# Shared places for the first expert's weights, the residual by the matrix unit and row stores ahead of the scan, in a two-layer kernel

## The reference, cut to what matters

```python
xn  = layernorm(x)                       # x: result of the first layer
x   = x + mamba(xn) + moe(xn)
mamba(r): y = scan over 1024 positions of h = exp(dt*A)*h + (dt*u)*B, y = sum(h*C), 16 states per channel
          return r + (y * silu(skip)) @ out_w.T          # r is the residual
moe(r):   logits = r @ gate_w + gate_b; two of 8 experts per token, softmax weights
          expert(r) = (silu(g) * h) @ w2 + b2 with h, g = split(r @ w1 + b1)
```

## Time and profile before

| | us |
|---|---|
| median of 3 runs (2567.91 to 2570.71) | 2570.66 |
| the profiled execution, its own time | 2571.51 |
| its span, first to last instruction | 2569.8 |
| DVE busy | 1967.2 |
| PE busy | 2128.3 |
| POOL busy | 1330.0 |

### The profile page before, as it was taken

The page is one execution under the profiler, slowest core; times in us unless marked ns, Lnnn a source line. Parts: engine busy times, 40 slices in busy tenths (PEclk is TensorE's granted clock), DMA queues, the critical chain, the costliest instruction groups (busy, mean ns, idle before and its releaser), DMA issues. The chain is left out here.

```text
span 2569.8 us, 34895 instructions
## 1 busy us (share of the span) xinstructions
PE 2128.3 (83%) x10642; PEld 1527.3 (59%) x10642; DVE 1967.2 (77%) x2692; ACT 1371.7 (53%) x2333; POOL 1330.0 (52%) x953
## 2 busy tenths in 40 slices
PE   2699999999976788788888888766599999999991
PEld 1578777787742233333333333332499999999991
DVE  6654566444536999989999999999498888888882
ACT  1322233322346766666666666743377777677760
POOL 1102222022224999999999999996024333433331
PEclk8899999999987999999999999999799999999996
DMA  8010011100121213131313131321466666666746
GB/s 263 17 42 16 25 41 41 41 25 16 41 74 59 103 62 113 66 109 74 113 60 116 61 112 62 105 82 66 173 226 220 208 230 233 217 210 227 236 138 206
DMA packets 117336, 290.84 MB, mean 113 GB/s; under 512 B 20788, under 2 KB 93892, under 8 KB 98452
## 3 DMA queue, kind: packets, MB, share of 16 engines
q1 hardware_dynamic: 102964, 271.31, 30.0%
q0 software_dynamic: 14304, 18.75, 3.6%
HBM read 239.21 MB, written 50.82 MB: 113 GB/s over the span
## 5 line engine op out<-in xcount | busy, mean ns | idle before, releaser
L1058 POOL TENSOR_TENSOR m_work<-m_ux,m_bb 128x1024 f32<-128x1024 f32 x256 | 601.7, 2370 | 37.3 <-DVE m_ux L1317 18.8
L1434 PE MATMUL m_y<-m_work,m_ident 128*128 128x512 f32 x1024 | 498.2, 609 | 1.5 <-DVE m_work L1347 1.5
L1204 ACT ACTIVATE m_da<-m_dl,m_A 128x512 f32<-128x512 f32 x512 | 347.9, 685 | 278.3 <-DVE m_hh L1339 277.5
L1748 PE MATMUL e_h<-e_xTh,e_w1h 128*128 128x256 f32 x1248 | 353.3, 283 | 17.1 <-DVE e_xTl L1684 17.1
L1748 PE MATMUL e_h<-e_xTl,e_w1h 128*128 128x256 f32 x1248 | 349.4, 280 | 0.0
L1748 PE MATMUL e_h<-e_xTh,e_w1l 128*128 128x256 f32 x1248 | 349.2, 280 | 0.0
L1347 DVE TENSOR_TENSOR m_work<-m_hh,m_cb 128x1024 f32<-128x1024 f32 x256 | 312.7, 1222 | 37.7 <-PE m_cb L1408 13.7
L1339 DVE TENSOR_TENSOR_SCAN m_hh<-m_da,m_carry,m_work 128x512 f32<-128x512 f32 x256 | 313.8, 1267 | 11.5 <-POOL m_work L1058 11.5
L1339 DVE TENSOR_TENSOR_SCAN m_hh<-m_da,m_work 128x512 f32<-128x512 f32 x256 | 298.4, 1207 | 14.7 <-POOL m_work L1058 14.5
L1434 PEld LDWEIGHTS m_y<-m_work,m_ident 128*128 128x128 f32 x1024 | 198.8, 194 | 161.8 <-issue 149.8
L281 POOL TENSOR_TENSOR small<-mv,eps_ln 128x4 f32<-128x4 f32 x17 | 3.4, 199 | 551.8 <-DVE mv L399 551.8
(11 more groups left out here) (263 smaller groups left out, 4755.9 us busy)
## 6 DMA issues: line engine op xcount, KB each, us to landing
e_w<-in_w SPq DMA_DIRECT2D x39, 2048.0 KB, 7.5
m_bb<-scratch_bT SPq DMA_DIRECT2D x64, 1024.0 KB, 4.6
e_w<-in_w SPq DMA_DIRECT2D x39, 1024.0 KB, 10.0
scratch_rec<-x1p SPq DMA_DIRECT2D x39, 260.0 KB, 8.1
e_xg<-scratch_rec SPq DMA_DIRECT2D x39, 260.0 KB, 2.7
e_b<-in_b SPq DMA_DIRECT2D x39, 128.0 KB, 3.0
xt<-in_x SPq DMA_DIRECT2D x9, 512.0 KB, 5.4
xres<-in_x SPq DMA_DIRECT2D x8, 512.0 KB, 4.8
```

The lines of the kernel that those rows point to most:

```text
L1058: pool.tensor_tensor(bx[:, u % NB], ux[q % 2][:, cols], slot.to_broadcast([P, HALF, T]), ALU.mult).then_inc(s_bx, 1)
L1204: act.activation(da[d % NA][:], dl[q % 2][:, e], ACT.Exp, scale=A[:, at:at + 1]).then_inc(s_exp, 1)
L1434: last = mm(y[:, i], ident[:], hc[:, u % 4, i], start=False, stop=(n % NST == NST - 1))
L1748: last = mm(hbank[m % HR][:, j], w[i][:, k, cols], x[i][:, k], start=(p == 0 and k == 0 and j == 0), stop=(p == 2 and k == KD - 1 and j == 1),
```

## The change

1. `mamba` places `xpad` and `w_si` in one tile `first`, which stays allocated for `experts`; the first expert tile's `w1` and `w2` take the same places. SP loads both at the end of `mamba`'s list, after their last reader. `experts` loads only rows, biases and the second tile's weights at its start.
2. The last output piece (O1 of chunk 7) goes to PSUM bank `da[0]` and to its own buffer `mo2`.
3. PE adds x1p to each output piece with an identity matmul; SP loads x1p for it (`load_res`) into the place of `xr`, so that the next `xr` is loaded later. `combine` becomes one copy from DRAM to DRAM.
4. The plan's exponential and matmuls move to slots (-2, 28) and (-2, 30). 14 of the 64 row stores come before the first step, the other 50 every fifth step.

```diff
+    PRE = 14
-        w_si = sb("w_si", [P, KD, 2 * E_IN])
+        first = dram["held"].enter_context(nc.sbuf_tensor("m_first", [P, KE * (PAD + 2 * T) + 2 * KD * E_IN], F32))
+        xpad = first[:, 0:KE * (PAD + 2 * T)].rearrange("p (e t) -> p e t", e=KE)
+        w_si = first[:, KE * (PAD + 2 * T):].rearrange("p (k n) -> p k n", k=KD)
+        xres = xr[:].rearrange("p k t -> p (k t)").rearrange("p (s d) -> p s d", d=D)
+            def load_res(p):
+                if p + 2 < NCH:
+                    wait_filled(sp, "SK3", p + 2)
+                if p > 0:
+                    wait_filled(sp, "O1", p - 1)
+                sp.dma_start(xres, dram["x1p"][p * T:(p + 1) * T, :].rearrange("(s p) d -> p s d", p=P)).then_inc(res_in, 16)
@@ SP, ahead of the steps
-            load_xr(1)
-            store_b(0)
             sp.wait_ge(s_d, D_STEPS)
...
+            sp.dma_start(tex0[:], dram["tex"][0:1, 0:1]).then_inc(tex0_in, 16)
             load_rows(0)
             load_rows(1)
+            load_xr(1)
+            store_b(0)
             load_b(0)
             load_b(1)
+            for j in range(2, PRE // TOPK + 1):
+                load_rows(j)
@@ SP, chunk q (load_rows becomes more_rows at the same places)
                 load_b(8 * q + 3)
-                load_rows(SUB * q + 2)
-                if q + 2 < NCH:
-                    load_xr(q + 2)
+                more_rows(32 * q + 0)
+                if q > 0:
+                    load_res(q - 1)
                 load_b(8 * q + 4)
                 if q > 0:
                     store_rows(q - 1, 0)
                     store_rows(q - 1, 1)
+                if q + 2 < NCH:
+                    if q > 0:
+                        wait_filled(sp, "O1", q - 1)
+                    load_xr(q + 2)
@@ SP, after the last chunk's list
+            sp.wait_ge(s_cv, NCH * KE)
+            wait_filled(sp, "SK3", NCH - 1)
+            sp.wait_ge(tex0_in, 16)
+            e = sp.value_load(tex0[0:1, 0:1], min_val=0, max_val=NE - 1)
+            sp.dma_start(first[:, 0:2 * KD * FF]..., dram["w1"][bass.ds(e * P, P), :, :]).then_inc(w_first, 16)
+            sp.dma_start(first[:, KE * (PAD + 2 * T):]..., dram["w2"][bass.ds(e * P, P), :, :]).then_inc(w_first, 16)
+            load_res(NCH - 1)
@@ POOL
-                    stores = [a // TOPK % 2 for a in range((q * NU + n + 2) // 4)]
+                    stores = [a // TOPK % 2 for a in range(PRE + (q * NU + n + 3) // 5)]
             pool.wait_ge(s_d, D_STEPS)
+            for a in range(PRE):
+                spread_rows(a)
             for u in range(AHEAD):
                 inputs(u)
-                if u % 4 == 2:
-                    spread_rows(u // 4)
+                if u % 5 == 2 and PRE + u // 5 < NPICK:
+                    spread_rows(PRE + u // 5)
@@ ACT and PE: the plan's parts
-                if (q, n) == (-1, 9):
+                if (q, n) == (-2, 28):
-                if (q, n) == (-1, 6):
+                if (q, n) == (-2, 30):
@@ PE, pieces O0 and O1
+                to = da[0] if (g, p) == ("O1", NCH - 1) else rb
                     pe.wait_ge(s_y1, 2 * p + 2)
+                    pe.wait_ge(res_in, 16 * (p + 1))
                     for s in (2 * j, 2 * j + 1):
+                        mm(to[:, at], ident[:], xres[:, s], start=(s % 2 == 0), stop=False, skip_group_check=True)
@@ experts
+            load_rows(0, 0)
             sp.dma_start(tex[:], dram["tex"]).then_inc(tex_in, 16)
...
             for t in range(2):
-                load_rows(t, t)
-                load_weights(t, t)
+                if t > 0:
+                    load_rows(t, t)
+                    load_weights(t, t)
+            act.wait_ge(w_first, 32)
+            dve.sem_inc(w_in[0], 16)
+            dve.sem_inc(w_in[0], 16)
@@ combine
+            sp.dma_start(out.rearrange("(p n) d -> p (n d)", p=P),
+                         dram["mo"][T:, :].rearrange("(p n) d -> p (n d)", p=P)).then_inc(out_done, 16)
```

More of the change, by code:

```diff
@@ L789, in mamba @@
         rb = ctx.enter_context(nc.psum_tensor("m_rb", [P, T], F32))
-        w_si = sb("w_si", [P, KD, 2 * E_IN])
+        dram["held"] = ExitStack()
+        first = dram["held"].enter_context(nc.sbuf_tensor("m_first", [P, KE * (PAD + 2 * T) + 2 * KD * E_IN], F32))
+        w_first = dram["held"].enter_context(nc.semaphore("m_w_first"))
+        dram["first"], dram["w_first"] = first, w_first
+        xpad = first[:, 0:KE * (PAD + 2 * T)].rearrange("p (e t) -> p e t", e=KE)
+        w_si = first[:, KE * (PAD + 2 * T):].rearrange("p (k n) -> p k n", k=KD)
+        tex0 = sb("tex0", [1, 1], I32)
+        tex0_in = sem("tex0_in")
         w_x = sb("w_x", [P, KE, DR + 2 * NST])
@@ L848, in mamba @@
         ps_before, ps_total = y[:, 0], y[:, 1]
+        res_in = sem("res_in")
         vec_in, w_si_in = sem("vec_in"), sem("w_si_in")
@@ L933, in _, with more_rows @@
             sp.wait_ge(s_out, 32)
+            sp.dma_start(tex0[:], dram["tex"][0:1, 0:1]).then_inc(tex0_in, 16)
             load_rows(0)
             load_rows(1)
+            load_xr(1)
+            store_b(0)
             load_b(0)
             load_b(1)
+            for j in range(2, PRE // TOPK + 1):
+                load_rows(j)
+            def more_rows(at):
+                for j in range(PRE // TOPK + 1, NJ):
+                    first = 5 * (TOPK * j - PRE) + 2
+                    if at + 8 <= first < at + 16:
+                        load_rows(j)
             for q in range(NCH):
@@ L1233, in _ @@
                 extra(u // NU, u % NU)
-            for j in range(2):
-                take_out(NCH - 1, j)
+            take_out(NCH - 1, 0)
+            wait_filled(act, "O1", NCH - 1)
+            act.activation(mo2, da[0][:].rearrange("p (s d) -> p s d", s=2), ACT.Copy).then_inc(drained, 1)
         @block.vector
@@ L1364, in piece @@
             def piece(g, p):
-                if turn[g, p] > 0:
+                to = da[0] if (g, p) == ("O1", NCH - 1) else rb
+                if turn[g, p] > 0 and to is rb:
                     pe.wait_ge(drained, turn[g, p])
@@ L1472, in experts @@
         tex = sb("tex", [1, NT], I32)
-        w1 = [sb(f"w1{i}", [P, KD, 2 * FF]) for i in range(2)]
-        w2 = [sb(f"w2{i}", [P, KF, D]) for i in range(2)]
+        first, w_first = dram["first"], dram["w_first"]
+        w1 = [first[:, 0:2 * KD * FF].rearrange("p (k n) -> p k n", k=KD), sb("w11", [P, KD, 2 * FF])[:]]
+        w2 = [first[:, KE * (PAD + 2 * T):].rearrange("p (k d) -> p k d", k=KF), sb("w21", [P, KF, D])[:]]
         w1h, w1l, w2h, w2l = ([sb(f"{n}{i}", shape, F32R) for i in range(2)] for n, shape in
@@ L1560, in _ @@
         def _(sp):
-            sp.dma_start(tex[:], dram["tex"]).then_inc(tex_in, 16)
-            sp.dma_start(texb[:], dram["tex"].to_broadcast([P, NT])).then_inc(texb_in, 16)
-            sp.wait_ge(tex_in, 16)
             def load_weights(t, i):
@@ L1780, in combine @@
     with ExitStack() as ctx:
-        def sb(name, shape, dt=F32):
-            return ctx.enter_context(nc.sbuf_tensor("c_" + name, shape, dt))
-        def sem(name):
-            return ctx.enter_context(nc.semaphore("c_" + name))
-        xa = sb("xa", [P, NJ, D])
-        mo = sb("mo", [P, NJ, D])
-        x_in = [sem(f"x_in{i}") for i in range(NCH)]
-        s_add, out_done = sem("add"), sem("out_done")
+        out_done = ctx.enter_context(nc.semaphore("c_out_done"))
         block = ctx.enter_context(nc.Block())
@@ L1794, in _ @@
         def _(sp):
-            for c in range(NCH):
-                for tile, src in ((xa, dram["x1p"]), (mo, dram["mo"][T:, :])):
-                    sp.dma_start(tile[:, c * SUB:(c + 1) * SUB], src[c * T:(c + 1) * T, :].rearrange("(s p) d -> p s d", p=P)).then_inc(x_in[c], 16)
-            for c in range(NCH):
-                sp.wait_ge(s_add, c + 1)
-                sp.dma_start(out[c * T:(c + 1) * T, :].rearrange("(s p) d -> p s d", p=P), xa[:, c * SUB:(c + 1) * SUB]).then_inc(out_done, 16)
-            sp.wait_ge(out_done, 16 * NCH)
-        @block.vector
-        def _(dve):
-            for c in range(NCH):
-                cs = slice(c * SUB, (c + 1) * SUB)
-                dve.wait_ge(x_in[c], 32)
-                dve.tensor_tensor(xa[:, cs], xa[:, cs], mo[:, cs], ALU.add).then_inc(s_add, 1)
+            sp.dma_start(out.rearrange("(p n) d -> p (n d)", p=P),
+                         dram["mo"][T:, :].rearrange("(p n) d -> p (n d)", p=P)).then_inc(out_done, 16)
+            sp.wait_ge(out_done, 16)
 def kernel(**inputs):
```

30 lines of the change are left out of this document (21 added, 9 removed).

## The result

The changed kernel takes 2539.78 us (median of four runs, 2537.77 to 2544.69) against 2570.53 us before (four runs). The ratio is 0.988, with a 95% interval from 0.9868 to 0.9892, so it is 1.1 to 1.3% faster. The forecast was 2530.8 us in a range from 2518 to 2548. The profiled execution took 2538.81 us, its span is 2537.0 us.

The account below looks back on a forecast made before the run. DVE was taken to pace mamba's steps, PE the experts, DMA the last window. Terms -16.6 - 12.4 - 10.4 - 2 + 1.5 = -39.9 us against 2571.51 gave 2531.6, 2530.8 as a median; range 2518 to 2548.

Parts of the forecast that it names:

- signs that the forecast had named against itself: Steps: PE waiting for x1p or over 20 us of broadcast waits; copy: last window under 15 or over 30 us.
- I take half of 423, 19.8 us, because each byte of a copy uses both sides: Combine: the 4.19 MB DRAM copy moves at half the first loads' 423 GB/s; 22.2 us with issue and landing, gain 16.6.
- The rival in which reading does not slow writing: Combine: copy at 423 GB/s takes 9.9 us, 12.3 instead of 22.2 in all, end at 2521; chance 0.2.
- Few engines, the slower rival: Combine: copy runs on few of 16 DMA engines; on one, 174 us, total 2685; chance 0.05.
- 0.1 us lost: Last output piece: four more matmuls cost 0.3 us more than the saved 0.69 us wait for ACT, less overlap.
- Four of this form take 1.03 us: Last output piece: time for the four matmuls that O0 and O1 together carry more.
- so I take 0.5 us back: Start of the experts: the second tile's weights are late next, costing 0.5 us of the 13.0 gain; bounds 0 to 4.
- of that stretch I take every POOL microsecond as one of the kernel's: Steps, step 26 to step 10 of the next chunk: nine fewer row stores at 1.16 us gain 10.4 us.
- lower bound of 0: Row stores in the steps: the gain of 10.4 us could be 0 if PE is last in their place.
- POOL next, which swallows most: Residual in the steps: DVE's following wait for POOL hides most of at most 7.2 us, leaving 1.5 us lost.
- at most 0.52 us: Residual on PE: cost of two added matmuls per output piece; 14 pieces in steps, at most 7.2 us.
- I estimate 0.8 us: Before the first step: delay of the chain to the first scan from PE's two plan matmuls ahead of SK0.

Follow-up runs that it names:

- e2: The changed kernel with all row stores back in the steps, every fourth step, none ahead of the first: 2538.17 us, ratio 0.9876 to the kernel before.
- e1: The changed kernel without the two residual matmuls of each output piece (x1p still loaded and waited for): 2530.35 us, ratio 0.9835 to the kernel before.
- e6: The changed kernel with three more row sets loaded ahead of the steps, so the 14 stores don't wait for row buffers: 2544.42 us, ratio 0.9889 to before.

## Why the forecast was right, and where it was not

The total lies 9 us above the forecast and inside the range, and that is in part luck: the copy came out 7.3 us better and nearly everything else worse. Two of the signs that the forecast had named against itself came about: more than 20 us of waits for the broadcast (25.6), and a last window under 15 us (14.95, though 15.1 to 15.5 in the other kernels with the whole copy).

**Combine: wrong in the rate, 7.3 us too slow.** The mis-sized term is "I take half of 423, 19.8 us, because each byte of a copy uses both sides". The copy runs at 328 to 355 GB/s in each direction, well above that half; the bytes take about 12 us and the start about 2.5, not 19.8 and 2.4. The rival in which reading does not slow writing, 9.9 us from the loads of the earlier trace rows, was nearer, and I had given it 0.2. The Trainium skill's 214 GB/s per direction, cited in the forecast, is not borne out: the measurement decides. The Trainium skill ("DMA: Bandwidth & Descriptors", Specifications) puts one core's share of DRAM at about 358 GB/s. The copy stays under that if one direction is counted, but the first loads ran at 423 GB/s, above it, so no run here shows that this limit is the cause; what sets the copy's rate stays open. Few engines, the slower rival, did not come about.

**Start of the experts: right, but 9.4 us in all and not 12.4, inside its bounds of 9 and 14.** The order of events and the 8.8 us to PE's start came as said, and undoing the early load alone gave back 13.7 us, where the forecast had 13.0. Two smaller terms were too small. "0.1 us lost" for the last pieces was 1.9: "Four of this form take 1.03 us" read four records of the earlier trace rows as four matmuls, but the trace shows each such matmul as two records (a piece of 8 has 16), so four more matmuls take 1.7 us. "so I take 0.5 us back" for the second tile's weights was 2.35, what the body lost, and issuing them 2 us earlier returned 2.1.

**Row stores: wrong in the step "of that stretch I take every POOL microsecond as one of the kernel's".** The waits for POOL did fall by 9.8 us, of 10.4 forecast. But DVE's waits for PE's broadcast rose by 11.9. DVE waits for whoever arrives last, and POOL was last by less than was taken off it. What the moved stores are worth depends on the rest: 6.0 us of the steps with whole pieces and no residual, 2.5 with halves, and 2.2 lost with whole pieces and the residual, each from single profiles that differ by up to 2 us. The fall of the waits is not the stores' alone either: with all stores back in the steps (e2) they are 18.8 us, not 26.0, for behind O0 and O1 (steps 11 and 14 of a chunk) DVE, held up by PE, no longer waits for POOL as it did in the kernel before. The forecast had a lower bound of 0 for this case ("if PE is last in their place"), but no rival and no chance of its own for it.

**Residual on PE: wrong in its size, and "POOL next, which swallows most" held only in the old rhythm.** The size has the same misreading as above: "at most 0.52 us" for a piece's two matmuls was 0.87, so 14 pieces carry 12.2 us and not 7.2. With the stores as in the kernel before, POOL did swallow it (e2). But the forecast added this term to the one that removes POOL's waits: with the moved stores it cost 4.5 us (e1), not 1.5. Two more things were not in the sum. First, the size of the burst matters and not only the work: a piece of 4.3 us behind y and broadcast matmuls of 2 us is more than a step of 3.9, and the same work in halves shows no cost. Second, the place of the clock's fall: the earlier trace rows showed O0 with PE at full clock, since the wait for POOL stood two steps earlier, and moving stores moved it.

**Before the first step: wrong sign, small.** POOL's first product began at 816.61, not 814.0. Two terms were mis-sized. The first store came at 791.24 and not 789.7, since the preparation ended 2.1 us later than before ("I estimate 0.8 us") and 0.3 us to issue came on top; and the last two stores took 3.3 us and not 2.3. The rounds between came as forecast: 8.1, 7.4 and 6.6 us, 22.1 in sum against 22.0, with 3.04, 2.08 and 1.68 us of waits for rows in them and row loads that landed in 1.8 to 2.5 us. The gain was not to be had by stores in any case. The first scans of the kernels with these 14 stores lie between 817.0 and 821.3. Without stores (e2) it was 819.8, with stores done early (e6) 820.6. POOL and DVE slow each other there when both are at work, which the forecast had seen in the earlier trace rows and did not carry on to the case of an early POOL. The Trainium skill ("SBUF — State Buffer", SBUF: two separate sides) describes a pair of ports that these two engines take in turn, one whole instruction at a time. The 3.25 us against 1.23 agree with that in kind, and no run here separates the ports from another cause. It is not so for every pair of operations: in the steps POOL multiplies nearly all the time (889.9 of 992.6 us busy), and DVE's multiplication by the broadcast (L1395), one of whose inputs lies in PSUM, takes 1.22 us.

**x1p and the weights in time: right.** No wait of PE for x1p in the steps, and the weights had landed.

## What to carry to other kernels

Before an engine's relief is counted, look at who arrives next and by how little: here 9.8 us off the waits for POOL came back as 11.9 us of waits for PE. Two terms that lean on the same waits can't be added: the residual was free while POOL's waits covered it, and the stores were worth something while PE had room. Work added to an engine that answers every step is priced by its longest burst against one step, so split it over steps before cutting it. A load known early is worth issuing into memory that both stages share (13.7 us for one weight set), and then the next load in the queue is the one to move.

## What the runs showed that was not expected

- A copy of 4.19 MB within DRAM took 14.6 to 15.1 us in eleven kernels, about 338 GB/s in each direction behind a start of 2.5 us, and with 1 KB rows (15.2 us) almost the same.
- After PE had stood 3.63 us, the granted clock was 0.55 for 3.4 us, and the two y matmuls behind it (four records) took 3.03 us instead of 1.72. A stall of PE is so paid twice where something waits for the matmuls behind it.
- The experts' body took 703.4 us in one profile, in which the row sums landed later (POOL's wait for them 297.7 us instead of 187.7), and 684.9 to 689.1 in all others. The same kernel run again had 688.2.
- POOL and DVE at once: 3.25 us instead of 1.23 for the same DVE operation, in the three kernels in which POOL's products started before 811 us (before, e2, e6), and in none in which they started later.
